# A decoder layer with routed experts: the last down matmuls of the shared expert and their addition moved behind the tile loop, the third chunk's addition moved behind the one-hots

## The reference

```python
shared = jax.nn.silu(xf @ Sg) * (xf @ Su) @ Sd
probs = jax.nn.softmax(xf @ Wr, axis=-1)
topk_p, topk_i = jax.lax.top_k(probs, K)
cw = jnp.zeros((T, n_exp), x.dtype).at[jnp.arange(T)[:, None], topk_i].add(topk_p)
...
    y = jax.nn.silu(xf @ wg) * (xf @ wu) @ wd
    return (acc + y * c[:, None], None)
...
return (routed + shared).reshape(b, s, d)
```

## Time and profile before

| | us |
|---|---|
| median of three runs | 588.15 |
| lowest and highest of them | 585.85, 589.64 |
| the profiled execution, its own time | 585.43 |
| its span, first to last instruction | 583.7 |
| TensorE busy in the span | 536.7 (92%) |
| VectorE, ScalarE, GpSimd busy | 376.6, 392.6, 213.0 |
| mean granted clock of TensorE, as a share of full speed | 0.983 |

### The profile page before, as it was taken

How to read it: one execution, slowest core, us unless ns; L and a number is a source line. 1 busy time by engine, 2 the same in 40 slices (tenths; PEclk the granted TensorE clock), 3 DMA queues, 4 the chain that set the end, 5 groups by cost and what they waited for, 6 DMA issues and landing times.

```text
span 583.7 us, 14119 instructions
## 1 busy us (share of the span) xinstructions
PE 536.7 (92%) x4519; PEld 290.7 (50%) x4520; DVE 376.6 (65%) x1017; ACT 392.6 (67%) x568; POOL 213.0 (36%) x238
## 2 busy tenths in 40 slices
PE   3985999999999999999999899999999989999990
PEld 2452333333333333333335577777666567777760
DVE  5797556566656656555555567887778974444495
ACT  4477999999999999999996356554524473333320
POOL 5000595099008920000000342345256643555551
PEclk9999899999999999999999999999999999999995
DMA  9933344344444444444431660000012233444686
GB/s 268 354 127 58 65 76 73 72 77 76 77 79 79 79 79 79 78 77 77 77 81 56 186 191 5 3 2 1 1 56 90 83 103 125 138 141 145 207 274 211
DMA packets 53547, 60.20 MB, mean 103 GB/s; under 512 B 10721, under 2 KB 44642, under 8 KB 53506
## 3 DMA queue, kind: packets, MB, share of 16 engines
q1 hardware_dynamic: 45986, 45.67, 32.9%
q0 software_dynamic: 3792, 10.36, 5.0%
q10 hardware_dynamic: 3728, 3.67, 1.9%
HBM read 22.17 MB, written 18.61 MB: 70 GB/s over the span
## 4 chain that ended last, share of the span: by engine, by line
PE 75%; DVE 7%; DMA 5%; ACT 5%; issue 3%; SPq 3%; POOL 1%; DVEq 0%; ACTq 0%; POOLq 0%
PE ps L721 20%; PE ps L732 20%; PE ps L1124 8%; PE ps L1141 3%; DMA x_slots<-val,place_i 3%; PE ps L765 2%; PE ps L1003 2%; PE ps L865 2%; PE ps L936 2%; PE ps L1116 2%; PE ps L648 2%; SPq L417 1%; SPq L419 1%; PE ps L883 1%; DVE ftmp L1802 1%
## 5 line engine op out<-in xcount | busy, mean ns | idle before, releaser
L1661 DVE TENSOR_TENSOR ps<-ps,kstack 128x128 f32<-128x128 f32 (+3 forms) x256 | 123.0, 492 | 96.2 <-PE ps L721 95.8
L1280 ACT ACTIVATE pT<-ps 128x1024 f32<-128x1024 f32 x128 | 125.4, 1034 | 6.1 <-PE ps L721 2.5
L721 PE MATMUL ps<-qstack,kstack 96*128 96x512 bf16 x352 | 93.0, 388 | 5.6 <-ACT kstack L1269 3.9
L732 PE MATMUL ps<-pT,vcur 128*32 128x256 f32 x1024 | 80.5, 387 | 0.0
L1280 ACT ACTIVATE xn<-ps 128x1024 f32<-128x1024 f32 x64 | 65.8, 1028 | 7.5 <-PE ps L721 7.3
L1280 ACT ACTIVATE xnT<-ps 128x1024 f32<-128x1024 f32 x64 | 65.9, 1030 | 0.2
L598 POOL DMA_INDIRECT y_tok<-ftmp,dest_i x47 | 45.1, 960 | 51.0 <-DVE ftmp L2124 50.4
L721 PEld LDWEIGHTS ps<-qstack,kstack 96*128 96x128 bf16 x352 | 27.4, 98 | 64.1 <-issue 31.2
L1124 PE MATMUL ps<-parts,xnT 128*128 x188 | 52.5, 402 | 3.0 <-ACT xnT L1452 2.6
L570 POOL TENSOR_TENSOR resid<-resid,projb 128x512 f32<-128x512 f32 x8 | 10.1, 1267 | 114.0 <-DVE xn L2033 113.4
L1457 ACT ACTIVATE oT<-ps 128x128 f32<-128x128 f32 x47 | 13.0, 277 | 54.1 <-PE ps L1124 52.3
(11 more groups left out here) (308 smaller groups left out, 942.7 us busy)
## 6 DMA issues: line engine op xcount, KB each, us to landing
qstack<-parts SPq DMA_DIRECT2D x132, 64.0 KB, 2.3
x_slots<-wcur SPq DMA_DIRECT2D x1, 6016.0 KB, 21.1
kT<-x_slots SPq DMA_DIRECT2D x47, 128.0 KB, 2.2
kstack<-parts SPq DMA_DIRECT2D x132, 32.0 KB, 2.0
early<-parts SPq DMA_DIRECT2D x60, 64.0 KB, 2.3
resid<-in_x_dram SPq DMA_DIRECT2D x4, 512.0 KB, 5.2
parts<-in_L_ffn_Wg_dram SPq DMA_DIRECT2D x16, 128.0 KB, 2.3
parts<-in_L_ffn_Wu_dram SPq DMA_DIRECT2D x16, 128.0 KB, 2.3
```

What stands on the lines that cost most here:

```text
L721: nc.tensor.matmul(ps[:, score_bank(g3, kt) + g, :], kstack[g3][:, kt * P:(kt + 1) * P], qstack[g3][:, 1 - first, 512 * g:512 * (g + 1)], ...
L732: mm = nc.tensor.matmul(out_g, vcur[:, r, kt, :], pT_ring[kt % 4].rearrange("p (t g q) -> p g t q", g=4, q=2 * HD)[:, g, :, :], start=(kt ...
L1280: nc.scalar.activation(pT_ring[kt % 4], two_banks(score_bank(g3, kt)).rearrange("p a n -> p (a n)"), ACT.Exp, bias=-SHIFT).then_inc(s_exp, 1)
L1661: nc.vector.tensor_tensor(blk, blk, within[:, side, 4 * P - n:] if side == 0 else within[:, side, 0:n], ALU.mult)\
```

## The change

On TensorE `down(3)` leaves its place behind `down(2)` and stands behind the last tile's down matmul. On VectorE the one-hots 20 to 31 come ahead of `accumulate(2)`, and `accumulate(3)` moves from there to the end, between the weighing of piece 2 and that of piece 3, with a wait for its own result. The waits for s_acc ahead of the tile steps ask for 3 in place of 4. Nothing is added or left out.

```diff
@@ -1079,7 +1079,6 @@
             gate_up(0, 3)
             gate_up(1, 3)
             down(2)
-            down(3)
 
             def destinations():
 
@@ -1166,12 +1165,13 @@
             pe.wait_ge(s_owner, 1)
             w_first = tile_weights(0)
             tile_gate_up(0, 0, w_first)
-            pe.wait_ge(s_acc, NCHUNK)
+            pe.wait_ge(s_acc, NCHUNK - 1)
             tile_steps(0, 4, {0: w_first})
             with pe.Fori(0, (SLOT_TILES - 7) // 8) as i:
                 tile_steps(8 * i + 4, 8, {})
             w_last = tile_steps(SLOT_TILES - 3, 3, {})
             tile_down(SLOT_TILES - 1, 2, w_last[2])
+            down(NCHUNK - 1)
 
@@ -2082,9 +2082,8 @@
             hidden(3, 0)
             hots(12, 20)
             hidden(3, 1)
+            hots(20, PAIRS)
             accumulate(2)
-            hots(20, PAIRS)
-            accumulate(3)
 
@@ -2105,7 +2104,7 @@
             dve.wait_ge(s_wtop, 1)
-            dve.wait_ge(s_acc, NCHUNK)
+            dve.wait_ge(s_acc, NCHUNK - 1)
 
@@ -2154,6 +2153,9 @@
             for c in range(NFIRST, NPIECE):
+                if c == NEARLY:
+                    accumulate(NCHUNK - 1)
+                    dve.wait_ge(s_acc, NCHUNK)
                 for r in range(TOPK):
                     weigh_from(c, r)
                     weigh(c, r, range(PIECES[c], PIECES[c + 1]))
```

## The result

The changed kernel takes 589.42 us (median of 20 runs, 586.88 to 591.58), the kernel before on the same chip 587.17 (20 runs, 584.42 to 589.88). The ratio is 1.0034, with a 95% interval of 1.0017 to 1.0050: 1.0 to 2.9 us slower, well under 1%. The prediction said 2.3 us slower, 590.0 us. Of the mechanism behind it one half was there (TensorE's clock falls) and one half was missed (a scatter of GpSimd is held up). The profiled execution took 589.7 us with a span of 587.9, 4.2 over the span of before.

The account below looks back on a forecast made before the run. The prediction took the scatter and load chain to bound the kernel ahead of the tile loop, and TensorE within it. Front 0, clock +2.3 and end 0 made 2.3 us slower, 590.0 us, range 585.5 to 594.0.

Parts of the forecast that it names:

- The front gains nothing: Ahead of the tile loop: the load still ends last, so down(3)'s 3.69 us off TensorE gain 0.
- the rival of a gain: Loop's head: quicker scatters let TensorE's chain end last; gain 0.2 us, at most 2.9, if the clock holds; chance 12%.
- destinations() from 474.5 to 476.0: TensorE ahead of the loop: destinations() waits only for the one-hots and ends 2.9 us before its present end.
- "GpSimd's scatters, SP's loads and ScalarE's copies stand where they stood, and none waits for an instruction that is moved.": Ahead of the loop: scatters, loads and copies keep their times, so the load's lateness and the front's gain of nothing stand.
- The clock falls, +2.3 us (0 to 6.8): Loop's head: idle TensorE drops to half clock between 476 and 481, until 484.7; 2.3 us lost, bounds 0 to 6.8.
- the forecast of 5.0: Loop's head: half clock lasts about 5.0 us after 479.68, taken from the earlier stretch at 52 to 62 us.
- the 0.4 us I counted: Loop's head: waits half speed doesn't lengthen, tile 2's load and 0.38 us of issue; half taken off the 2.5 us loss.
- The end, 0 (0 to 0.2): Behind the last tile: down(3) and its addition hide in VectorE's wait for y_tok, about 1.1 us over; cost 0 to 0.2.
- The sum: Whole kernel: front 0, clock +2.3, end 0, so 2.3 us slower, 590.0 us; chance of 1.5 to 3.5 slower 60%.

Follow-up runs that it names:

- f3: The kernel before with three scatters of GpSimd in flight in place of two: 585.46 us, ratio 0.9972 to the kernel before.
- f4: The changed kernel with three scatters of GpSimd in flight in place of two: 586.17 us, ratio 0.9965 to the kernel before.
- e1: The changed kernel with sixteen unread filler matmuls where down(3) had stood, ahead of destinations(): 590.89 us, ratio 1.0038 to the kernel before.
- e2: The changed kernel with twelve unread filler matmuls behind destinations(), in TensorE's pause: 589.29 us, ratio 1.0006 to the kernel before.
- e4: The changed kernel with down(3) and its addition left out altogether: 590.41 us, ratio 1.0027 to the kernel before.
- e3: The kernel before with only VectorE's one-hots 20 to 31 moved ahead of accumulate(2), down(3) staying: 589.84 us, ratio 1.0018.
- d1: The changed kernel with the run of one-hots 20 to 31 issued a second time, unread: 602.07 us, ratio 1.0083 to the kernel before.
- x1: The changed kernel with accumulate(2) back ahead of the one-hots 20 to 31: 598.69 us, ratio 1.0030 to the kernel before (596.83 us in that job).
- x2: The changed kernel with accumulate(2) back ahead of the one-hots 20 to 31, timed in a later job: 588.77 us, ratio 1.0018.
- b1: The changed kernel with VectorE's old order and sixteen filler matmuls at down(3)'s old place with its old wait: 588.85 us, ratio 1.0016.
- f1: The kernel before with four scatters of GpSimd in flight in place of two: 606.65 us, ratio 1.0161 to the kernel before.
- f2: The changed kernel with four scatters of GpSimd in flight in place of two: 604.0 us, ratio 1.0121 to the kernel before.

## Why the prediction was right, and where not

- **The front gains nothing.** Right. The scatters and the load end last in both kernels, and 3.69 us taken off TensorE bring no earlier start of the loop. f3 and f4 show the condition from the other side: with quicker scatters the gain appears in the profile, 1.7 us, inside the bound of 2.9 that the rival of a gain set, though not in the medians.
- **destinations() from 474.5 to 476.0.** Right: 474.56 to 476.13.
- **"GpSimd's scatters, SP's loads and ScalarE's copies stand where they stood, and none waits for an instruction that is moved."** This is the step that failed. No semaphore ties a scatter to a one-hot, but the scatter at 472.41 was held until the run of one-hots was over, and the load that releases TensorE came 2.1 us later. Of the five profiles with the new order, the run as it is and two scatters in flight, four (the changed one, e1, e2, e4) have such a scatter, of 2.93, 3.01, 3.03 and 3.01 us; in the fifth, e3, the scatters came at other moments, and the longest was 1.81. d1 shows with a doubled run that the run's length sets it. The old order isn't free of it: in x1, x2 and b1 the last scatter was held for 1.74, 1.73 and 1.49 us, and in each it ended 0.83 us after the run. A row of before hid it: there a scatter started at 474.82, inside the run, and took 1.11 us. I read from the earlier trace rows that the two overlap, and took their overlap as free.
- **The clock falls, +2.3 us (0 to 6.8).** The mechanism is right: low from 476.2 to 486.4, forecast as a stretch that begins between 476 and 482 and ends by 488. The term was mis-sized. It is 1.2 us in the profile. Half speed was in force for 4.6 us of the loop's head (481.80 to 486.4), near the forecast of 5.0, but that head held more waits than the 0.4 us I counted: in before, 2.87 us pass from the first gate and up matmul to the third tile's (484.31 less 481.44) with gaps in them, and in the changed kernel they became 3.83, not 5.7. Twelve profiles give the same two values for this stretch (the table above). And part of the pause was itself due to the held scatter (5.67 us where 3.7 were forecast).
- **The end, 0 (0 to 0.2).** Right. VectorE waits 1.39 us behind the addition, forecast 1.1; e4, without down(3) and the addition, is no faster by more than the noise (1.0027 against 1.0034). The profiles are sharper: from the last tile's down to the end of the span 13.2 to 14.6 us pass in the nine profiles with down(3) there (mean 13.9), and 13.6 to 13.9 in the five without it (before, e3, e4, f1, f3; mean 13.8).
- **The sum.** Forecast +2.3 us against +2.0 in the timed runs, 1.0 to 2.9. In the profiled execution +4.2: 2.1 from the late load, some 1.8 of it the held scatter's; 1.2 from the clock; 0.9 from the loop and the last loads, which no run ties to the change. That the forecast fits so well is luck in part: one term was missing and one was too large.

What stays open: how much of the timed 2.0 us belongs to the scatter and how much to the clock. The intervals of e2, e3, x2 and b1 all hold both no loss and nearly the full one, and the medians pull both ways: e1 is 1.6 us over e2 in the same job, though both have the long hold, and b1 and x2 are equal, though only x2 has the low clock. Open too is why some scatters inside a run of one-hots are held (2.93 us at 472.41 in the changed kernel) and others aren't (1.11 at 474.82 in before; 0.96 at 474.44 in x2, 0.98 at 473.82 in e3, each followed by one that is held). Before has one profile only, so whether its scatters are often held, as the last ones of x1, x2 and b1 are, isn't known; if they are, the change adds less than the 1.8 us of the profiled pair.

## What to carry to other kernels

Before work is moved on VectorE, look at which GpSimd instructions run in the new place, not only at who waits for whom: a DMA that GpSimd issues can be held by VectorE's run without any semaphore between them, and if that DMA is on the chain, the rest of the run is too. If TensorE waits for a transfer at a place, taking work from TensorE there buys only a longer pause, and the pause is paid for again in the clock; shorten the transfer's chain first (with three scatters in flight in place of two both kernels took 0.3% less than the kernel before).

## What the runs showed of the hardware

**A run of vector instructions holds a scatter.** The duration of the held scatter follows from the run's end: 474.50 and 475.34 in the changed kernel, 485.64 and 486.46 in d1. Each single one-hot is only 0.31 us long. One long instruction seems to do it too: beside the comparison of 128x1504 elements, 1.72 us, which also reads two operands in SBUF (L1976; L1975 in e4), scatters took 1.91, 1.91 and 1.90 us in e3, e4 and x2, and each ended 0.82 to 0.83 us after the comparison. The Trainium skill, in "SBUF — State Buffer", section "Who interferes with whom", says that a VectorE instruction with two SBUF inputs contends with a GpSimd instruction that reads SBUF, and calls the contention an exclusive lock in which the order of issue decides who blocks. The one-hots read two (jidx, high_low), so the rule points at the right pair. By it alone a scatter would, as an estimate, be late by one instruction of 0.31 us; these runs show it late by the rest of the run, 2 us and, in d1, 4.8.

**Engines that stand still while scatters are in flight.** In the job of x1, d1, f1 and f2 all four profiles had VectorE and ScalarE idle before 455 us, for 9.40 and 6.84 us in x1, labelled remote, and GpSimd waited 9.2 to 11.6 us ahead of its scatter at 460.7 to 462.9 (1.86 in the changed kernel, ahead of the one at 452.30); with four in flight they stood still again, 9.61 and 14.24 us in f1. The kernel before took 596.83 us in that job, and 587.54 in a later one on the chip of the same number. What releases the engines the trace doesn't show, and whether four in flight would cost as much without these waits wasn't tried.

**The clock's stretches don't all depend on the change.** In the changed kernel, e1, e3 and x2 the clock is also low for 3.4 to 6.9 us from some 322 on, in before, e2, e4 and b1 it isn't. From 52 to 70 the mean granted clock is 0.81 in before, e3 and e4 and 0.72 in the changed kernel, e1, e2, x2 and b1. Neither cost anything that can be seen further on: the scatter at 458 starts at 458.12 in the changed kernel and at 458.04 in before.
